# A state cast and half of the xnT evacuations go from VectorE to ScalarE in a fused gated-slot-attention and channel-mixing layer

## The reference, cut to what matters

```python
xn = layernorm(x)                                  # eps 1e-5
# attention: H=4 heads, K=V=256, M=64 slots
q, k, v = swish(xn@Wq), swish(xn@Wk), xn@Wv
f = log_sigmoid(xn@Wf) / 8;  s = 1 - exp(f)
for t:                                             # recurrence over tokens
    hk = hk*exp(f_t) + k_t (x) s_t                 # [H, K, M]
    p  = softmax(q_t*K**-0.5 . hk)                 # [H, M]
    hv = hv*exp(f_t) + s_t (x) v_t                 # [H, M, V]
    o_t = p . hv
attn = (o * rsqrt(mean(o*o) + 1e-5) * g) @ Wo
# channel mixing, x_prev is xn one token before
xr, xk = mu_r*xn + (1-mu_r)*x_prev, mu_k*xn + (1-mu_k)*x_prev
ffn = sigmoid(xr@W_r) * (relu(xk@W_k)**2 @ W_v)
out = x + attn + ffn
```

## Time and profile before

| | us |
|---|---|
| two timed runs | 1889.56 and 1912.45, median 1901.01 |
| profiled execution | 1893.29 |
| span of its slowest core (core 7) | 1891.8 |
| spans of the eight cores | 1882.1 to 1891.8 |
| PE busy, DVE busy, ACT busy (core 7) | 1293.9, 813.5, 512.3 |

### The profile page before, as it was taken

One profiled execution on the slowest core, in us unless ns is written; L12 is line 12 of the kernel. 1 busy time (PEld: TensorE's weight loads), 2 busy tenths in 40 slices (PEclk: granted clock), 3 DMA queues, 4 the chain that ended last, 5 costly groups with the idle time before them and its releaser, 6 DMA issues.

```text
span 1891.8 us, 22926 instructions; the slowest of 8 cores (1882.1 to 1891.8 us)
## 1 busy us (share of the span) xinstructions
PE 1293.9 (68%) x8172; PEld 781.4 (41%) x8172; DVE 813.5 (43%) x1857; ACT 512.3 (27%) x1105; POOL 43.4 (2%) x80
## 2 busy tenths in 40 slices
PE   2407596866859586685958668596866859586774
PEld 1203263544426253442635444263544426253442
DVE  2334435345353534535353453535345353535433
ACT  1102232322223222222323222232322223232322
POOL 0000000000000000000000000000000000000000
PEclk9756596877959687795958779595877959687786
DMA  6770000000000000000000000000000000000000
GB/s 182 245 246 23 11 12 33 13 23 23 23 12 12 34 12 23 23 23 12 12 32 13 23 23 23 12 12 34 12 23 23 23 12 12 34 12 23 23 1 23
DMA packets 19135, 65.76 MB, mean 35 GB/s; under 512 B 2256, under 2 KB 3664, under 8 KB 19024
## 3 DMA queue, kind: packets, MB, share of 16 engines
q0 software_dynamic: 12736, 47.19, 7.1%
q1 hardware_dynamic: 6288, 17.12, 2.6%
HBM read 47.52 MB, written 16.78 MB: 34 GB/s over the span
## 4 chain that ended last, share of the span: by engine, by line
PE 53%; DVE 22%; ACT 9%; issue 7%; DMA 5%; DVEq 1%; SPq 0%; ACTq 0%; POOL 0%; POOLq 0%
PE pB L167 18%; PE pA L167 16%; PE pC L167 8%; PE pF L167 5%; DVE hv L828 3%; PE pD L167 3%; PE pT L172 2%; PE pE L167 2%; DVE lnscr L296 2%; ACT xn_bf L886 2%; DVE xn_bf L335 1%; DVE hv_bf L833 1%; DVE fstage L583 1%; DVE tmp L578 1%; ACT L500 1%
## 5 line engine op out<-in xcount | busy, mean ns | idle before, releaser
L167 PE MATMUL pC<-wo_sb,xn_bf 128*128 128x512 bf16 x256 | 111.6, 614 | 28.5 <-ACT xn_bf L886 28.5
L661 ACT ACTIVATE t_l<-t_e,t_linv 128x256 f32<-128x256 f32 x32 | 16.3, 510 | 374.7 <-DVE t_linv L644 374.7
L167 PE MATMUL pA<-wrt_sb,fstage 128*128 128x512 bf16 x256 | 62.5, 389 | 67.4 <-DVE xtail L468 67.4
L172 PE MATMUL pT<-identb_sb,xn_bf 128*128 128x128 bf16 x256 | 32.4, 306 | 92.3 <-DVE xnT L359 66.5
L492 DVE TENSOR_TENSOR Am_sb<-pD,mask_sb 128x512 bf16<-128x512 f32 x16 | 11.1, 692 | 178.8 <-PE pD L167 178.7
L167 PE MATMUL pD<-v_sb,spp 128*64 128x256 bf16 x64 | 19.6, 410 | 96.7 <-ACT o_bf L800 96.7
L507 DVE CAST l_hi<-t_l 128x512 bf16<-128x512 f32 x16 | 6.8, 426 | 183.3 <-ACT t_l L503 183.3
L172 PE MATMUL pT<-identb_sb,k_sb 128*128 128x128 bf16 x256 | 32.4, 267 | 75.4 <-ACT kT_sb L675 75.4
L905 DVE TENSOR_TENSOR ob<-pC,fstage 128x512 f32<-128x512 f32 x32 | 22.1, 691 | 136.6 <-PE pC L167 136.6
L167 PE MATMUL pA<-wvt_sb,xnT 128*128 128x512 bf16 x256 | 61.1, 382 | 24.3 <-DVE xnT L534 16.6
L886 ACT COPY xn_bf<-pT 128x512 bf16<-128x512 bf16 x64 | 34.5, 589 | 157.5 <-PE pT L172 157.3
(11 more groups left out here) (162 smaller groups left out, 2649.6 us busy)
## 6 DMA issues: line engine op xcount, KB each, us to landing
out<-ob POOLq DMA_DIRECT2D x32, 512.0 KB, 2.9
xb<-x POOLq DMA_DIRECT2D x30, 512.0 KB, 4.1
stage<-wq POOLq DMA_DIRECT2D x2, 1024.0 KB, 8.0
fstage<-wq SPq DMA_DIRECT2D x2, 1024.0 KB, 8.1
fstage<-wk SPq DMA_DIRECT2D x2, 1024.0 KB, 6.7
stage<-wk POOLq DMA_DIRECT2D x2, 1024.0 KB, 5.8
fstage<-wv SPq DMA_DIRECT2D x2, 1024.0 KB, 6.1
stage<-wv POOLq DMA_DIRECT2D x2, 1024.0 KB, 6.4
```

Source lines behind the costliest of these rows:

```text
L167: e.matmul(out=o, lhsT=l, rhs=r, start=st, stop=sp),
L172: lambda e, o=out_ap, i=in_ap, d=ident: e.transpose(out=o, in_=i, identity=d),
L661: em("scalar", lambda e: e.activation(out=sm_e, in_=sm_lg, func=AF.Exp, scale=SCALE, bias=nmS4[:, 0:1]), waits=[("V", nms_done)], inc="S")
```

## The change

Two pieces of work change the engine. The cast of hk_sb to hk_bf becomes an ACT copy (L788), which is appended in emit_R_hb at the same place, and the logits of the next chunk wait for S in place of V. And in emit_P0_trans the tile r = 1 of each j is copied to xnT by ACT (L365), the tile r = 0 still by DVE (L359); the token shift in emit_P (L452) gets a wait for S besides. The gate of pF now stands behind the addition to hk_sb in place of the cast.

```diff
-        hkbf_done = [0]
+        hkbf_done = [("S", 0)]
...
                     dst = xnT[:].rearrange("p (i jj t) -> p i jj t", i=8, jj=2)[:, r * 4:(r + 1) * 4, j, :]
-                    if evac_eng == "vector":
+                    if r == 0:
                         em("vector", lambda e, d=dst, b=bank: e.tensor_copy(
...
             em("vector", lambda e: e.tensor_copy(out=xnprevT[:, 1:2048], in_=xnT[:, 0:2047]),
-               waits=[("V", allw), CONSTS])
+               waits=[("V", allw), CONSTS, ("S", xnT_doneS)])
...
-                        wi = ([("V", hkbf_done[0])] if (h == 0 and ii == 0) else ())
+                        wi = ([hkbf_done[0]] if (h == 0 and ii == 0) else ())
...
-            em("vector", lambda e: e.tensor_copy(out=hk_bf[:], in_=hk_sb[:]),
-               waits=[("V", val("V"))], inc="V")
-            hkbf_done[0] = val("V")
             reader(pF, "V")
+            em("scalar", lambda e: e.copy(out=hk_bf[:], in_=hk_sb[:]),
+               waits=[("V", val("V")), ("S", val("S"))], inc="S")
+            hkbf_done[0] = ("S", val("S"))
```

## The result

| | before | after |
|---|---|---|
| median, us | 1893.55 (10 runs) | 1934.34 (11 runs) |
| ratio, 95% interval | | 1.0206 (1.0176 to 1.0237) |
| profiled execution, us | 1893.29 | 1934.10 |
| span of the slowest core, us | 1891.8 | 1932.6 (core 0) |

The account below looks back on a forecast made before the run. No engine is full; a relay of handovers through PE, DVE and ACT bounds the kernel. 28.6 + 2.7 + 1.0 + 6.9 = 39.2 us on the profiled 1893.3 gave 1932.5, range 1915 to 1948.

Parts of the forecast that it names:

- cast of chunk 1: Ahead of the first wo loop: ACT's waiting cast delays both oT copies by 1.79 us, 28.6 us over 16 superchunks.
- cast of chunk 0: At the state handover to chunk 1: the cast takes about 0.60 us on ACT, not 0.43; 2.7 us in all.
- xnT copies: At the last o transposes before the second wo loop: ACT's second copy delays them; 0.07 x 15 = 1.0 us.
- The large term: The cast of chunk 1, queued on ACT ahead of both oT copies: 28.6 us, bounds 27.8 to 31.0.
- rival 4: Faster by relief of DVE, which loses 26.6 us of xnT copies and casts: 1866.7 us; chance 0.03.
- rival 3: At the first wo loop the delay is swallowed, leaving only 2.7 + 1.0 us: 1897 us; chance 0.07.
- The clock term: In the wo loops: PE's longer empty stretch makes its clock rise later, +6.9 us, bounds -13 to +22.5.
- The three quarters: For the clock: three quarters of the way from the mean superchunk distance to 110.67 us, 0.46 x 15 = 6.9 us.
- rival 1: In the wo loops the clock doesn't mind; only 32.3 us count: 1925.6 us, down to 1915; chance 0.28.
- The range's low end: For the whole kernel: 1915 us, taken from the low end of rival 1, with the clock rising early.
- static terms: The two casts and the xnT copies, without the clock: 28.6, 2.7 and 1.0, together 32.3 us.
- the wait for hk_bf in superchunk 7: Sign at the first chunk: PE's wait for hk_bf, 2.72 us before, should be 2.9 in the changed kernel.

Follow-up runs that it names:

- The doubled cast: The changed kernel with ACT's hk_bf cast of chunk 1 made twice in a row, same data and target: 1934.37 us, ratio 1.0234 to the kernel before the change.

## Why the prediction was right

1932.5 was forecast and 1934.34 measured. By its own steps:

| term | forecast, us | measured, us | by |
|---|---|---|---|
| cast of chunk 1 | 16 x 1.79 = 28.6 | 14 x 1.88 + 2 x 2.23 = 30.8 | transposes to wo loop, 3.80 or 4.15, less 1.92 |
| cast of chunk 0 | 16 x 0.17 = 2.7 | 16 x 0.23 = 3.7 | hk_sb to logits, 1.59 - 1.36 |
| xnT copies | 15 x 0.07 = 1.0 | 15 x 0.09 = 1.4 | transposes to wo loop, 1.98 - 1.89 |
| clock | 6.9 | 6.1 | wo loops, 192.6 - 186.5 |
| sum | 39.2 | 42.0 | against 40.8 |

- Whether the kernel is slower by over 2%, to which I gave 0.50, isn't settled by the measurement.
- The large term and its mechanism hold: with the cast out of the way of the oT copies, by either of two ways, 27 to 30 us go. It was 0.09 too small in each superchunk. The handover from DVE to ACT is 0.04 longer than that to DVE itself (0.83 to 0.84 from start to start against 0.79), and the hold is 0.52, not 0.48. The first is at the casts' place for chunk 0 too, where a cast of 0.618 in place of my 0.60 adds the rest of the 0.06.
- The Trainium skill's page ScalarE: Activation LUTs, section What ACT_TABLE_LOAD costs, gives, by the estimate in the prediction, 613 ns and a hold of 520. The cast measures 618 and 520; I had set it aside for rows of casts that read PSUM, at 0.59 and 0.48. With the page the term would have been 29.3, nearer. The measurement decides for the page.
- The relief of DVE was worth nothing (rival 4): the kernel is no faster anywhere, and the split alone is 1.0021. The reason I gave there, that the copies that move have ended before PE asks for them, holds for the first of the two alone; the second is on the way of the last o transposes, as my own term for it had it. The delay wasn't swallowed either (rival 3).
- The clock term has the right size for a reason that doesn't hold. I took it as positive since an emptier stretch ahead of the loop would make the rise late. The doubled cast made the stretch emptier by 0.70, and the loops took 10.1 us less. With the cast behind oT or back on DVE the stretch was 0.88 again, as before the change, and the loops still took 191.4 and 191.3 us, against 192.6 with the change and 186.5 before it. So the step that failed is "an emptier stretch ahead of the loop speaks for a later rise". What the runs show in its place is that small changes of the times ahead of the loops, that of the cast of chunk 0 among them, put the rise at another place in them, within 182.5 to 192.6 us of loop time, and that work in the stretch brings it ahead of the first loop in most superchunks (156.6). What sets the place is open. The three quarters by which I came to 6.9 were a choice, so that the sum came out is in part luck, and rival 1 (1925.6) would have been as well founded.
- The range's low end doesn't follow from my own bounds: 32.3 of static terms and -13 of clock give 1912.5, not 1915. And the wait for hk_bf in superchunk 7 was to be 2.9 and is 2.58; over all superchunks it grew by the 0.23 of the table.
- Why the distances are nearly the same, 112.6 and 112.8, whether one cast or two stand ahead of oT, isn't settled: the loop times show that the clock gives back 10.1 of the 11.2 us, not why just so much.

## What to carry to other kernels

Before moving work to an idle engine, look at what stands behind it in that engine's queue. Behind its idle time an instruction may stand that is soon ready, and a moved one whose own wait is still open blocks it: here a cast of 0.6 us cost 1.9 in each superchunk, and nothing once it stood behind the two copies. Where PE works in bursts between handovers, read its loops' busy time beside the shifts, as it shows what the clock took or gave, and a delay in one place can be given back in another. And look what could fill PE's waits: first useful work that can be moved there (2.5% here), then matmuls that nobody reads (8.8% for both together).

## What the runs showed of the hardware

- A delay of 0.70 us in each superchunk, 11.2 in all, made the distance between superchunks only 0.2 longer and left no difference that the times could show, as PE's clock rose earlier within the loops behind it, which took 10.1 us less.
- Five filling matmuls of 128x512 at the lower level (2.34 us) ahead of the first wo loop of each superchunk saved 37 us in 16 superchunks: the busy time of all wo loops went from 192.6 to 156.6 us.
- With the waits filled, the mean granted clock of the cores is 0.94 in place of 0.76 and the time 5.6% less, though the chain holds no less work. A wait of 2.5 us left open ahead of the loop was followed by a loop at the lower level, 3.55 us in place of 1.89, and cost 46 us (1878 against 1832).
- Filling that outlasts its wait delays the relay: nine matmuls took 4.00 us with the clock down and 2.11 with it up, and the logits behind them came 3.04 and 1.59 us after hk_sb.
